# Early-fusion block on one core: queries, keys and values read back in two halves, and a new order of all engines

## The chip, the cores and the metric

The kernel runs on one core of one Trainium2 chip. The metric is the device time of one execution in microseconds (us). The core has five engines with a queue of instructions each: TensorE (PE: matmuls; its weight loads are PEld), VectorE (DVE), ScalarE (ACT), GpSimd (POOL) and SyncE (SP). In this kernel SP issues every DMA, all on one hardware queue (q1), and nothing else. An engine works through its instructions in the order written and waits on semaphores; one late instruction holds up all behind it.

## The reference, cut to what matters

```
for each of 64 images x (3, 224, 224) and texts txt (77, 256):
    p = 196 patches of 16 x 16 x 3 = 768 numbers
    h = layernorm(layernorm(p) @ W(768, 256) + b)        # 196 tokens
    h = concat(h, txt)                                   # 273 tokens of 256
    y = layernorm(h);  q, k, v = y Wq', y Wk', y Wv' + biases     # 256 each
    q, k, v of an image are split by reshape/transpose into n = 16 heads of d = 16:
        scores = einsum('nqhd,nkhd->nhqk', Q, K) / 4
        # h is a token position here: each token has its own 16 x 16 table over heads
    o = softmax(scores) V;  h = h + reshape(o) Wo' + bo
    z = layernorm(h);  z_prev = z shifted by one token
    out = h + sigmoid(mix_r(z, z_prev) Wr') * (relu(mix_k(z, z_prev) Wk')^2 Wv')
```

The attention is thus a small 16 x 16 problem for each of the 17,472 tokens, with the 16 heads as rows. All data is float32; the large products are made from a rounded part and a remainder ("hi" and "lo", three matmuls for each of two halves of the 256 inputs: six in a product).

## The kernel before, in words

The 64 images are worked on in 16 groups of four (a quad). A quad has 1092 tokens, and these are cut into three chunks of 364 tokens (CPQ = 3), each held as three tiles of 126, 126 and 112 rows (TOK, TILES). Image stages (patches to tokens) run once an image, the others once a chunk.

Everything is one software pipeline. The table AT gives each kind of step a number of due times, in units of a schedule in which a quad is 12,000 units, an image 3,000 (PERIOD of IMAGE_OPS) and a chunk 4,000. Each engine's body walks through all due times in rising order (STEPS) and issues what is due, for whichever quad it belongs to (`due`). So AT is nothing but the order of the instructions on each engine: a due time starts nothing, semaphores do. BANK says which of the eight PSUM banks each TensorE step writes; `turn` makes the step wait for the last reader of the step before it on that bank.

The steps that matter here, for a chunk k, with their names in AT and their lines:

- `qkv` (line 1066 through `product`): six products, two for each tile, into PSUM; `qb` (line 866, DVE) adds the bias and writes them to the tile qkvt.
- `qkv_out` (line 526, SP): three DMAs, one a tile, each when its two `qb` are done, from qkvt to qkv_dram in DRAM.
- `qk_in` (line 532, SP): one DMA of 768 KB reads queries and keys back, 128 bytes at a time, in an order in which partitions hold (token, head). Before it SP waits until all three tiles have landed in DRAM (`after_all(qkv_out, ...)`) and until the steps of the chunk before have read the tile qk.
- `v_in` (line 542, SP): eight DMAs of 48 KB read the values back, 64 bytes at a time.
- `kspread` (line 954, ACT, four instructions) and `qplace` (line 852, DVE, two) read the whole tile qk; then `s` (line 1103, PE, two parts) makes the scores. `mx`, `sub` (DVE), `exp` (ACT), `pt` (line 1111, PE), `ptc` (ACT), `av` (line 1124, PE; it needs all eight `v_in`), `rec`, `osb` (line 777, DVE) follow.
- `o_out` (line 547, SP): nine DMAs write the result of a chunk to o_dram; `o_in` (line 556, SP): four DMAs read it back as rows, after `o_out` of the same chunk and, for the first two chunks of a quad, of the next one has landed. `ont` (line 1180, PE) transposes the rows, `wo` multiplies.
- Other steps on SP's queue: `load` (line 495, an image), `txt` (508), `hdma` (519: three or four DMAs, the patch tokens to their place), `out` (563).
- Other steps on PE: `x` (1134), `tok` (1146), `stat` (1153), `xt` (1162), `zt` (1194), `k`, `r`, `val`, `wo` (all 1066).

The order on SP around the read-back, in the middle chunk window (due times 4653 to 7932) is: qkv_out of tile 0, out x2, txt, load, qkv_out of tile 1, o_out, qkv_out of tile 2, hdma, o_in, qk_in, out, v_in.

Of the kernel before, what the change touches and what calls it, by code (L numbers as in the profile page):

```python
# [25 lines left out]
HEADS, HD = 16, 16  # L26
IPQ, CPQ = 4, 3
QUADS = IMAGES // IPQ
# [4 lines left out]
TILES = 3  # L33
PT = 98
QKV = 3 * HD
# [6 lines left out]
BLK = 24  # L42
CTP = 16 * BLK
GR = 2 * BLK
RUN = 48
PARTS = 2
# [3 lines left out]
VROW = 5 * HD  # L50

SLOT, IMG, QUAD = 4000, 3000, 12000
AT = dict(load=[0], xcols=[1318, 1320, 1583], sq=[3246], ssq=[3924], sqm=[3700, 4330], x=[2170, 2293, 2490],
    xh=[2282, 2545, 2674], xl=[2509, 2936, 2943], tok=[3277, 4254], stat=[4432], statc=[4602], statr=[4742],
    rstd1=[4804], txt=[8554], yn=[5075, 5247], st2=[6518, 6589], mv2=[6765, 6814], rstd2=[7194], hg=[6861, 7595],
    h=[7598, 7865], hdma=[9448], st3=[12882, 13196, 13294], mv3=[13054, 13295, 13379], rstd3=[13763], xn=[14260,
    14279, 14449], xt=[14661, 15107], xnh=[14950, 15196], xnl=[15072, 15505], hb=[16159], qkv=[15721, 15888, 16255,
    16593, 16786, 17092], qb=[15897, 15942, 16599, 16651, 16997, 17149], qkv_out=[16653, 18001, 18379],
    qk_in=[18794], v_in=[19932], qplace=[19665, 19706], kspread=[19343, 19395, 19463, 19541], s=[20021, 20045],
    mx=[20102, 20201], sub=[20221, 20230], exp=[20322, 20464], pt=[20333, 20499], ptc=[20595, 20603, 20609, 20634],  # L60
    av=[20708, 20712], rec=[20736, 20809], osb=[20791, 20828], o_out=[22086], o_in=[26611], ont=[26722, 26748],
    onh=[26894, 26987], onl=[26996, 27109], wo=[27468, 27507, 27713], h2=[27696, 27736, 27802], st4=[28277, 28291,
    28297], mv4=[28302, 28428, 28473], rstd4=[28576], z=[28737, 28819, 28831], zt=[28864, 28875], carry=[27865],
    ztc=[29110, 29174], d=[29450, 29454], edge=[29465], mix=[29564, 29767, 30411, 30536], mixh=[29773, 30169, 31589,
    31775], mixl=[30115, 30183, 32095, 32294], k=[30531, 30872], kr=[30870, 31114], ksq=[30967, 31291], kah=[31781,
    32685], kal=[32727, 33437], r=[32763, 33240, 33705], rt=[32972, 33579, 33931], val=[33604, 33790, 34157],
    rv=[33858, 33944, 34175], add=[34793, 35351, 35382], out=[35541, 37270, 37274], sqh=[3466])

BANK = dict(x=[5, 3, 1], tok=[3, 1], stat=[5], yn=[7], xt=[2, 0], qkv=[0, 5, 0, 2, 5, 0], s=[4, 2], pt=[4, 6],
    av=[4, 6], ont=[5, 4], wo=[4, 6, 2], zt=[4, 6], k=[0, 6], r=[0, 2, 2], val=[0, 5, 0])  # L70
# [116 lines left out]
def fusion_kernel(nc, x, txt, ln1_g, ln1_b, tok_w, tok_b, ln2_g, ln2_b, wq, bq, wk, bk, wv, bv, wo, bo,  # L187
                  w_r, w_k, w_v, mu_r, mu_k, out):
    with ExitStack() as ctx:
# [3 lines left out]
        def sig(name, per, primed=False, unit=1):  # L193
            return Signal(ctx, nc, name, per, CPQ, primed, unit)
# [19 lines left out]
        xcols = sb("xcols", [XROWS, GRID * 128])  # L214
# [3 lines left out]
        rstd1 = sb("rstd1", [PT, 2])  # L218
# [4 lines left out]
        mv2 = sb("mv2", [PT, 2, 2])  # L223
# [20 lines left out]
        osb = probs  # L244

        mx = sb("mx", [128, BLK // 4 * 8])
# [4 lines left out]
        z = sb("z", [TT, TILES, E])  # L251
# [4 lines left out]
        kr = dT  # L256
# [3 lines left out]
        r = sb("r", [TT, TILES, E])  # L260
# [6 lines left out]
        qkv_dram = nc.dram_tensor("qkv_dram", (CPQ, CTP, HEADS, QKV), F32, kind="Internal").ap()  # L267
# [7 lines left out]
        prep_pool = ctx.enter_context(nc.semaphore("prep_pool"))  # L275
# [32 lines left out]
        st3 = sig("st3", 3)  # L308
# [5 lines left out]
        xn_lo = sig("xn_lo", 2)  # L314
        qkv_pe = sig("qkv_pe", 6, True)
        qkv_sb = sig("qkv_sb", 6)
        qkv_out = Own(ctx, nc, "qkv_out", [TILES] * CPQ, 16)
        qk_in = sig("qk_in", 1, True, unit=16)
        v_in = sig("v_in", 8, True, unit=16)
        hb_sb = sig("hb_sb", 1, True)  # L320
        q_sb = sig("q_sb", 2, True)
        kb_sb = sig("kb_sb", 4, True)
# [6 lines left out]
        av_pe = sig("av_pe", PARTS, True)  # L329
# [48 lines left out]
        def place(kind, j):  # L378
            return banks[BANK[kind][j]]

# [73 lines left out]
        def _(sp):  # L454
# [25 lines left out]
            def after(signal, q, k, steps):  # L480
                signal.wait(sp, q, k, steps)
                settle(sp)

            def after_all(own, q, k):
                own.wait(sp, q, k)
                settle(sp)

            def body(q):
                for s in STEPS:
# [30 lines left out]
                    for i, (o, rows) in enumerate(TOK):  # L520
                        for k in due(q, s, "qkv_out", i):
                            after(qkv_sb, q, k, 2 * i + 2)
                            if i == 0:
                                after(qk_in, q, k - CPQ, 1)
                                after(v_in, q, k - CPQ, 8)
                            qkv_out.done(k, sp.dma_start(qkv_dram[k % CPQ, o:o + rows, :, :].rearrange("t i j -> t (i j)"), qkvt[0:rows, i, :]))
                    for k in due(q, s, "qk_in", 0):
                        after_all(qkv_out, q, k)
                        after(kb_sb, q, k - 1, 4)
                        after(q_sb, q, k - 1, 2)  # L530
                        src = qkv_dram[k % CPQ, :, :, 0:2 * HD]
                        qk_in.done(sp.dma_start(qk[:, :, :], src.rearrange("(g t) i j -> (t i) g j", t=8)))
                    for k in due(q, s, "v_in", 0):
                        if q * CPQ + k == 0:
                            sp.wait_ge(prep_pool, POOL_ALL)
                        after_all(qkv_out, q, k)
                        after(av_pe, q, k - 1, PARTS)
                        src = qkv_dram[k % CPQ, :, :, 2 * HD:QKV].rearrange("(r g y) i j -> r y i g j", r=2, y=4)
                        for rr in range(2):
                            for yy in range(4):  # L540
                                p = 64 * rr + HEADS * yy
                                v_in.done(sp.dma_start(vb[p:p + HEADS, :, yy, 0:HD], src[rr, yy]))
# [21 lines left out]

            quads(sp, body)
            out_dma.wait(sp, QUADS - 1, CPQ - 1, 3)
            qk_in.wait(sp, QUADS - 1, CPQ - 1, 1)
            v_in.wait(sp, QUADS - 1, CPQ - 1, 8)
            on_in.wait(sp, QUADS - 1, CPQ - 1, ROW_DMAS)

# [135 lines left out]
        def _(dve):  # L706
# [42 lines left out]
            def body(q):  # L749
                for s in STEPS:  # L750
# [93 lines left out]
                            mv3_sb.done(V.bn_aggr(mv3[0:rows, i, :], bn3[0:rows, i, :]))  # L844
                    for xx in range(2):
                        for k in due(q, s, "qplace", xx):
                            qk_in.wait(dve, q, k, 1)
                            s_pe.wait(dve, q, k - 1, PARTS)
                            settle(dve)
                            half = slice(64 * xx, 64 * xx + 64)  # L850

                            q_sb.done(V.tensor_reduce(qx[half, :, xx, :], qk[half, :, 0:HD].unsqueeze(3), AX.X, ALU.max))  # L852
# [4 lines left out]
                    for job in range(6):  # L857
                        for k in due(q, s, "qb", job):
                            i, half = job // 2, job % 2
                            rows = TOK[i][1]  # L860
                            qkv_pe.wait(dve, q, k, job + 1)
                            if job == 0 and q * CPQ + k == 0:
                                dve.wait_ge(prep_act, ACT_ALL)
                            if job == 0:
                                qkv_out.wait(dve, q, k - 1)
                            qkv_sb.done(V.tensor_tensor(qkvt[0:rows, i, NQ * half:NQ * half + NQ], place("qkv", job)[0:rows, 0:NQ],  # L866
                                                        bqkv[0:rows, :, :].rearrange("p i j -> p (i j)")[:, NQ * half:NQ * half + NQ], ALU.add))

# [48 lines left out]
        def _(act):  # L917
# [319 lines left out]
```

## Time and profile before

| | us |
|---|---|
| median of 3 runs | 1610.56 (1608.76 to 1613.27) |
| the profiled execution's own time | 1609.15 |
| its span, first to last instruction | 1607.4 |

| engine | busy us | share of the span |
|---|---|---|
| PE | 1450.4 | 90% |
| PEld | 1378.2 | 86% |
| DVE | 1264.3 | 79% |
| ACT | 1113.4 | 69% |
| POOL | 947.0 | 59% |

The profile's page gives busy times of each engine, their course over the span, the DMA queues, the chain of work that ended last, and groups of like instructions with the idle time of the engine before them and what ended it ("releaser"). "issue" as a releaser means that nothing the profile shows was waited for.

### The profile page before, as it was taken

Reading aid. Unit: us, or ns where it says so; the run is one execution under the profiler, and the core shown is the slowest. Engines: PE = TensorE matmul, PEld = TensorE weight load, DVE = VectorE, ACT = ScalarE, POOL = GpSimd, SP = SyncE. Lnnn points to the kernel's source line nnn. Section 1 sums busy time; section 2 is a strip of 40 time slices with the busy share of each in tenths; the row PEclk is TensorE's granted clock in tenths of the full one; section 3 lists DMA queues with packets and bytes.
Section 4 is the critical chain, followed back from the end, with each engine's and each line's share of the span. In section 5 each row is a group of like instructions: output and inputs, shape, how many; then the busy total and the mean of one; then the engine's idle time right before and its main releaser. Section 6 shows DMA issues by size and latency. Waiting matters only on the chain.

```text
span 1607.4 us, 53715 instructions
## 1 busy us (share of the span) xinstructions
PE 1450.4 (90%) x18762; PEld 1378.2 (86%) x18762; DVE 1264.3 (79%) x3171; ACT 1113.4 (69%) x2230; POOL 947.0 (59%) x1428
## 2 busy tenths in 40 slices
PE   4687899999989999998999899999999999897866
PEld 4676899899989999898989899998988999897755
DVE  5566798888888888887988688888888788886753
ACT  4554687777777787776777678777777777765643
POOL 3342376566667666565667566666766566664546
PEclk8788899999999999999999999999999999999998
DMA  5267987997878887987888798798888689868760
GB/s 140 63 125 126 139 154 147 150 159 158 151 144 162 157 156 154 149 152 145 155 147 157 140 151 154 162 150 147 155 158 156 137 152 148 160 123 127 123 100 29
DMA packets 702660, 227.67 MB, mean 142 GB/s; under 512 B 617470, under 2 KB 673854, under 8 KB 702394
## 3 DMA queue, kind: packets, MB, share of 16 engines
q1 hardware_dynamic: 702394, 224.23, 77.3%
q8 instruction: 153, 2.51, 0.8%
q14 instruction: 113, 0.93, 0.3%
HBM read 121.64 MB, written 89.64 MB: 131 GB/s over the span
## 4 chain that ended last, share of the span: by engine, by line
PE 65%; SPq 8%; issue 6%; DMA 5%; DVE 3%; POOL 1%; ACT 1%; DVEq 0%; POOLq 0%; ACTq 0%
PE bank L1066 33%; PE bank L1146 13%; PE bank L1103 4%; PE bank L1124 4%; SPq L547 4%; DMA qk<-qkv_dram 3%; PE bank L1134 3%; SPq L519 2%; PE bank L1111 2%; PE bank L1180 2%; PE bank L1162 1%; PE bank L1194 1%; DMA on<-o_dram 1%; SPq L556 1%; PE bank L1153 1%
## 5 line engine op out<-in xcount | busy, mean ns | idle before, releaser
L1066 PE MATMUL bank<-wqkv,xnT 128*126 128x384 f32 (+1 forms) x1728 | 357.8, 347 | 6.9 <-issue 6.8
L1146 PE MATMUL bank<-wtok,xT 128*98 128x258 f32 x2304 | 315.7, 293 | 13.3 <-DVE xT L789 9.3
L1146 PEld LDWEIGHTS bank<-wtok,xT 128*98 128x98 f32 x2304 | 294.8, 172 | 18.9 <-DVE xT L789 11.3
L1066 PEld LDWEIGHTS bank<-wqkv,xnT 128*126 128x126 f32 (+1 forms) x1728 | 293.6, 186 | 10.6 <-issue 8.0
L689 POOL TENSOR_TENSOR mixp<-mixf,mixp 128x364 fp32r<-128x364 f32 x192 | 185.5, 977 | 166.0 <-ACT mixp L1040 158.7
L866 DVE TENSOR_TENSOR qkvt<-bank,bqkv 126x384 f32<-126x384 f32 (+1 forms) x288 | 156.0, 550 | 83.5 <-PE bank L1066 83.4
L954 ACT ACTIVATE arena<-qk,ymask 128x768 f32<-128x768 f32 x192 | 164.0, 926 | 57.1 <-DMA qk<-qkv_dram 56.9
L637 POOL TENSOR_TENSOR xcols<-xcols 84x896 f32<-84x896 f32 x59 | 124.9, 2117 | 86.9 <-ACT xcols L996 86.3
L987 ACT ACTIVATE xT<-bank 128x420 fp32r<-128x420 f32 (+1 forms) x192 | 100.5, 536 | 61.7 <-PE bank L1134 59.9
L1066 PE MATMUL bank<-wrT,mixp 128*126 128x256 f32 (+1 forms) x864 | 134.3, 292 | 4.8 <-POOL mixp L689 2.9
L979 ACT ACTIVATE xcols<-xim 84x640 f32<-84x640 f32 (+1 forms) x192 | 126.5, 694 | 12.9 <-DVE xs L784 12.0
L626 POOL TENSOR_TENSOR rs<-ve,small 126x3 f32<-126x3 f32 (+1 forms) x160 | 127.7, 798 | 12.5
L852 DVE TENSOR_REDUCE qx<-qk 64x768 f32<-64x768 f32 x96 | 90.8, 945 | 54.2 <-DMA qk<-qkv_dram 52.7
L899 DVE SCALAR_TENSOR_TENSOR mixf<-dT,mus,bank 128x364 f32<-128x364 f32 x192 | 110.1, 584 | 21.3 <-POOL dT L683 17.1
L1066 PE MATMUL bank<-mixp,wkfT 128*128 128x364 f32 x576 | 120.3, 345 | 5.6 <-POOL mixp L689 5.0
L1066 PEld LDWEIGHTS bank<-wrT,mixp 128*126 128x126 f32 (+1 forms) x864 | 114.8, 186 | 10.2 <-POOL mixp L689 3.8
L1066 PE MATMUL bank<-wvfT,kaT 128*126 128x256 f32 (+1 forms) x864 | 121.9, 285 | 1.2 <-DVE r L911 0.9
L1134 PE MATMUL bank<-ident,xcols 84*128 84x84 f32 x896 | 100.4, 246 | 24.1 <-DVE bank L808 13.0
L1066 PE MATMUL bank<-woT,onT 128*126 128x256 f32 (+1 forms) x864 | 117.3, 287 | 2.2 <-DVE onT L872 2.2
L642 POOL TENSOR_TENSOR var<-stat,mean 98x2 f32<-98x2 f32 x64 | 12.6, 197 | 176.4 <-DVE stat L799 176.4
L966 ACT ACTIVATE pt<-bank 64x384 f32<-64x384 f32 x192 | 93.1, 485 | 33.1 <-PE bank L1111 29.6
L677 POOL TENSOR_TENSOR dT<-zT 128x364 f32<-128x364 f32 x96 | 74.1, 794 | 69.5 <-ACT zT L1034 69.5
(125 smaller groups left out, 3328.4 us busy)
## 6 DMA issues: line engine op xcount, KB each, us to landing
xim<-in_x SPq DMA_DIRECT2D x128, 294.0 KB
qk<-qkv_dram SPq DMA_DIRECT2D x48, 768.0 KB, 7.7
qkv_dram<-qkvt SPq DMA_DIRECT2D x96, 378.0 KB
arena<-qkv_dram SPq DMA_DIRECT2D x384, 48.0 KB
qkv_dram<-qkvt SPq DMA_DIRECT2D x48, 336.0 KB
o_dram<-probs SPq DMA_DIRECT2D x288, 48.0 KB, 1.8
out<-h SPq DMA_DIRECT2D x96, 126.0 KB
on<-o_dram SPq DMA_DIRECT2D x64, 126.0 KB
```

What stands on the lines that cost most here:

```text
L626: done.done(P.tensor_tensor(rs[:, :], ve[:, :], powt[0:part, 0:ve.shape[1]], ALU.pow))
L637: x_half.done(P.tensor_tensor(halves[:, 0, :, :], halves[:, 0, :, :], halves[:, 1, :, :], ALU.add))
L689: mix_lo.done(P.tensor_tensor(mixp[:, w, 1, kk, :], mixf[:, kk, :], mixp[:, w, 0, kk, :].bitcast(F32), ALU.subtract))
L866: qkv_sb.done(V.tensor_tensor(qkvt[0:rows, i, NQ * half:NQ * half + NQ], place("qkv", job)[0:rows, 0:NQ], bqkv[0:rows, :, :].rearrange("p ...
L899: mix_sb.done(V.scalar_tensor_tensor(out=mixf[:, kk, :], in0=dT[:, kk, :], scalar=mus[:, w, kk:kk + 1], in1=place("zt", kk)[:, 0:CT], op0= ...
L954: kb_sb.done(A.activation(kb[:, :, yy, :], qk[:, :, HD:2 * HD], ACT.Copy, scale=ymask[:, yy:yy + 1]))
L966: pt_sb.done(A.activation(pt2[64 * rr:64 * rr + 64, PB * part:PB * part + PB, :, rr, :], place("pt", part)[64 * rr:64 * rr + 64, 0:32 * PB ...
L979: x_cols.done(A.activation(xcols[:, 128 * w0:128 * w1].rearrange("p (w r q) -> p w r q", r=HALF, q=PS), xim[:, :].rearrange("p (r w q) -> ...
L987: x_hi.done(A.activation(xT[:, 0, :, w0:w1], src, ACT.Copy))
L1066: ins = mm(psum, left(a, k), right(b, k), start=t == 0, stop=t == len(terms) - 1)
L1134: ins = tr(place("x", job)[:, XROWS * (w - w0):XROWS * (w - w0) + XROWS], xcols[:, 128 * w:128 * w + 128], ident[0:XROWS, 0:XROWS])
L1146: ins = mm(place("tok", c)[0:PT, 0:E + 2], xT[:, a, i0:i0 + GRID // 2, :].rearrange("p i w -> p (i w)"), wtok[:, b, ch, :], start=t == 0, ...
```

## The change

Four edits, and one that goes over everything:

1. The signal of the write-out is split: qkv_out counts tiles 0 and 1, a new qkv_end counts tile 2.
2. `qk_in` becomes two DMAs of 384 KB, with a due time each. The first reads tokens 0 to 191 of the chunk and waits only for tiles 0 and 1 (tokens 0 to 251) in DRAM; the second reads the rest and waits for tile 2 too. `kspread` and `qplace` wait for both.
3. `v_in` becomes two steps of four DMAs each, with the same waits.
4. `qb` of the next chunk waits for qkv_end as well.
5. Every due time in AT and nearly every bank in BANK is another. On SP the read-back is now, in the middle chunk window (4643 to 7126): qkv_out of tile 0, txt, qkv_out of tile 1, o_out, qkv_out of tile 2, qk_in first half, o_in, qk_in second half, hdma, load, v_in first half, out, v_in second half. On TensorE, from `av` of a chunk to the `ont` of the chunk before it, the order is r0, qkv4, zt, qkv5, x and r1, val0, r2, val1, val2, tok, k0, xt0, ont in this window before; it is qkv4, r0, qkv5, zt, x and r1, r2, val0 to val2, tok, k0, xt0, xt1, k1, ont after. From qkv5 to the first `s` of the same chunk both orders hold two tok, stat, three val, two r, one image's x, two k, two xt, two ont and two qkv; before there are also three wo, after two wo and two zt.

```
-    st3=[12882, 13196, 13294], ... qkv=[15721, 15888, 16255, 16593, 16786, 17092],
-    qb=[15897, 15942, 16599, 16651, 16997, 17149], qkv_out=[16653, 18001, 18379],
-    qk_in=[18794], v_in=[19932], qplace=[19665, 19706], kspread=[19343, 19395, 19463, 19541], s=[20021, 20045],
-    ... av=[20708, 20712], rec=[20736, 20809], osb=[20791, 20828], o_out=[22086], o_in=[26611], ont=[26722, 26748],
+    st3=[11805, 11903, 12190], ... qkv=[14573, 14584, 14947, 15304, 15637, 16016],
+    qb=[14667, 14706, 15296, 15397, 15916, 16032], qkv_out=[16643, 17110, 17292],
+    qk_in=[17362, 17672], v_in=[18137, 19126], qplace=[18505, 18524], kspread=[18429, 18432, 18448, 18484], s=[18755, 18760],
+    ... av=[19360, 19636], rec=[19684, 19745], osb=[19748, 19752], o_out=[21202], o_in=[25473], ont=[26050, 26162],
...
-        qkv_out = Own(ctx, nc, "qkv_out", [TILES] * CPQ, 16)
-        qk_in = sig("qk_in", 1, True, unit=16)
+        qkv_out = Own(ctx, nc, "qkv_out", [2] * CPQ, 16)
+        qkv_end = Own(ctx, nc, "qkv_end", [1] * CPQ, 16)
+        qk_in = sig("qk_in", 2, True, unit=16)
...
-                            qkv_out.done(k, sp.dma_start(...))
-                    for k in due(q, s, "qk_in", 0):
-                        after_all(qkv_out, q, k)
-                        after(kb_sb, q, k - 1, 4)
-                        after(q_sb, q, k - 1, 2)
-                        src = qkv_dram[k % CPQ, :, :, 0:2 * HD]
-                        qk_in.done(sp.dma_start(qk[:, :, :], src.rearrange("(g t) i j -> (t i) g j", t=8)))
-                    for k in due(q, s, "v_in", 0):
-                        ...
-                        for rr in range(2):
+                            (qkv_out if i < 2 else qkv_end).done(k, sp.dma_start(...))
+                    for rr in range(2):
+                        for k in due(q, s, "qk_in", rr):
+                            after_all(qkv_out, q, k)
+                            if rr:
+                                after_all(qkv_end, q, k)
+                            else:
+                                after(kb_sb, q, k - 1, 4)
+                                after(q_sb, q, k - 1, 2)
+                            src = qkv_dram[k % CPQ, CTP // 2 * rr:CTP // 2 * rr + CTP // 2, :, 0:2 * HD]
+                            qk_in.done(sp.dma_start(qk[:, BLK * rr:BLK * rr + BLK, :], src.rearrange("(g t) i j -> (t i) g j", t=8)))
+                        for k in due(q, s, "v_in", rr):
+                            ...
+                            after_all(qkv_out, q, k)
+                            if rr:
+                                after_all(qkv_end, q, k)
+                            else:
+                                after(av_pe, q, k - 1, PARTS)
...
-                            qk_in.wait(dve, q, k, 1)
+                            qk_in.wait(dve, q, k, 2)
...
+                                qkv_end.wait(dve, q, k - 1)
...
-                                qk_in.wait(act, q, k, 1)
+                                qk_in.wait(act, q, k, 2)
```

## Rows read from the trace of the kernel before

**Rows 1.** The page's head and its first part: busy us (share) xinstructions.
```profile
span 1607.4 us, 53715 instructions
...
PE 1450.4 (90%) x18762; PEld 1378.2 (86%) x18762; DVE 1264.3 (79%) x3171; ACT 1113.4 (69%) x2230; POOL 947.0 (59%) x1428
```
**Rows 2.** Busy time by stretch: start, middle and end of the run, columns in the first line.
```profile
core 0: us, PE busy (x) PEld busy (x) DVE busy (x) ACT busy (x) POOL busy (x), PEclk, DMA share, GB/s
0.00:200.00 200.00, 143.31 (x1422) 134.51 (x1423) 123.95 (x298) 101.25 (x185) 68.83 (x124) 0.85 0.63 119
200.00:1400.00 1200.00, 1144.29 (x15319) 1094.20 (x15318) 1013.26 (x2563) 898.37 (x1805) 764.78 (x1137) 0.99 0.84 152
1400.00:1608.00 208.00, 162.82 (x2023) 149.47 (x2022) 127.13 (x312) 113.81 (x242) 113.43 (x168) 0.95 0.58 104
```
**Rows 3.** Waits of PE, 200 to 1400 us: waiting <- releaser: us, times, longest.
```profile
PE bank L1180 <- DMA on<-o_dram: 17.5, 12, 2.2
PE bank L1103 <- issue: 16.9, 21, 2.5
PE bank L1124 <- issue: 6.3, 5, 3.7
```
**Rows 4.** The chain that ended last, 700 to 760 us: start us, us, what.
```profile
722.28 0.99 PE bank L1124 x46
...
725.16 0.31 SPq L547
...
728.84 0.42 SPq L547
729.38 0.36 SPq L526
729.99 0.79 SPq L519
...
734.38 0.33 SPq L556
...
735.61 2.11 DMA on<-o_dram
737.76 0.85 PE bank L1180 x6
```
**Rows 5.** SP's timeline, 686 to 725 us: start us, us, engine line op out<-in xcount.
```profile
699.81 0.35 SPq L526 DMA_DIRECT2D qkv_dram<-qkvt  x1
...
701.06 1.47 SPq L556 DMA_DIRECT2D on<-o_dram  x4
702.79 0.40 SPq L532 DMA_DIRECT2D qk<-qkv_dram  x1
```
**Rows 6.** What reads and writes the tile qk, 200 to 1400 us: durations, landing.
```profile
L954 ACT ACTIVATE arena<-qk,ymask x159: 917/922/945, 199.6 to 1395.2; 128x768 f32<-128x768 f32 x159
...
DMA to landing us min/median/max: 6.9/7.7/9.1
```
**Rows 7.** The chain that ended last, whole run: lengths of TensorE steps.
```profile
396.64 2.15 PE bank L1146 x18
398.79 2.82 PE bank L1066 x24
```
**Rows 8.** The chain that ended last, 1470 to 1540 us (the end of the run).
```profile
1478.29 7.49 DMA qk<-qkv_dram
...
1493.60 1.05 PE bank L1066 x6
...
1501.62 2.77 DMA qkv_dram<-qkvt
1504.62 7.13 DMA qk<-qkv_dram
...
1531.73 7.36 DMA qk<-qkv_dram
```
**Rows 9.** The page's DMA issues: KB each, median us from issue to landing.
```profile
o_dram<-probs SPq DMA_DIRECT2D x288, 48.0 KB, 1.8
```

More of the change, by code:

```diff
@@ L52 @@
 SLOT, IMG, QUAD = 4000, 3000, 12000
[L53 to L58, printed above, removed]
-    qk_in=[18794], v_in=[19932], qplace=[19665, 19706], kspread=[19343, 19395, 19463, 19541], s=[20021, 20045],
[L60 to L67, printed above, removed]
@@ L69 @@
-BANK = dict(x=[5, 3, 1], tok=[3, 1], stat=[5], yn=[7], xt=[2, 0], qkv=[0, 5, 0, 2, 5, 0], s=[4, 2], pt=[4, 6],
-    av=[4, 6], ont=[5, 4], wo=[4, 6, 2], zt=[4, 6], k=[0, 6], r=[0, 2, 2], val=[0, 5, 0])
+AT = dict(load=[0], xcols=[520, 575, 1066], sq=[2536], ssq=[3118], sqm=[3504, 3521], x=[1147, 1315, 1348], xh=[1421,
+    1534, 1605], xl=[1448, 1769, 1827], tok=[2216, 3215], stat=[3306], statc=[3506], statr=[3613], rstd1=[3700],
+    txt=[7688], yn=[4137, 4156], st2=[5150, 5471], mv2=[5563, 5770], rstd2=[6383], hg=[5727, 6031], h=[6728, 6763],
+    hdma=[8728], st3=[11805, 11903, 12190], mv3=[12254, 12268, 12276], rstd3=[12632], xn=[13144, 13351, 13481],
+    xt=[13692, 13813], xnh=[14049, 14278], xnl=[14107, 14384], hb=[15441], qkv=[14573, 14584, 14947, 15304, 15637,
+    16016], qb=[14667, 14706, 15296, 15397, 15916, 16032], qkv_out=[16643, 17110, 17292], qk_in=[17362, 17672],
+    v_in=[18137, 19126], qplace=[18505, 18524], kspread=[18429, 18432, 18448, 18484], s=[18755, 18760], mx=[18861,
+    18872], sub=[18895, 18925], exp=[18987, 18991], pt=[19233, 19257], ptc=[19242, 19347, 19413, 19415], av=[19360,
+    19636], rec=[19684, 19745], osb=[19748, 19752], o_out=[21202], o_in=[25473], ont=[26050, 26162], onh=[26402,
+    26403], onl=[26434, 26441], wo=[26666, 26669, 26764], h2=[26729, 26735, 26999], st4=[26993, 27168, 27178],
+    mv4=[27220, 27370, 27373], rstd4=[27544], z=[27683, 27999, 28012], zt=[28056, 28139], carry=[26769], ztc=[28231,
+    28367], d=[28462, 28467], edge=[28473], mix=[28600, 28704, 29385, 29598], mixh=[28788, 29167, 29790, 30510],
+    mixl=[29008, 29318, 30623, 30661], k=[29621, 29919], kr=[29913, 30290], ksq=[30095, 30339], kah=[30632, 30820],
+    kal=[31056, 31667], r=[31922, 32308, 32469], rt=[32103, 32591, 32942], val=[32785, 32962, 33004], rv=[32834,
+    33076, 33162], add=[33724, 34252, 34312], out=[34720, 35795, 36432], sqh=[2880])
@@ L71 @@
+BANK = dict(x=[5, 1, 3], tok=[1, 3], stat=[5], yn=[7], xt=[5, 6], qkv=[6, 0, 4, 6, 0, 2], s=[5, 0], pt=[2, 0],
+    av=[2, 4], ont=[4, 0], wo=[4, 2, 6], zt=[6, 4], k=[0, 2], r=[5, 0, 2], val=[5, 0, 2])
 BANK_ORDER = ("s", "pt", "av", "x", "tok", "stat", "xt", "qkv", "ont", "wo", "zt", "k", "r", "val", "yn")
@@ L523, in body @@
                             if i == 0:
-                                after(qk_in, q, k - CPQ, 1)
+                                after(qk_in, q, k - CPQ, 2)
                                 after(v_in, q, k - CPQ, 8)
-                            qkv_out.done(k, sp.dma_start(qkv_dram[k % CPQ, o:o + rows, :, :].rearrange("t i j -> t (i j)"), qkvt[0:rows, i, :]))
-                    for k in due(q, s, "qk_in", 0):
-                        after_all(qkv_out, q, k)
-                        after(kb_sb, q, k - 1, 4)
-                        after(q_sb, q, k - 1, 2)
-                        src = qkv_dram[k % CPQ, :, :, 0:2 * HD]
-                        qk_in.done(sp.dma_start(qk[:, :, :], src.rearrange("(g t) i j -> (t i) g j", t=8)))
@@ L533, in body @@
-                    for k in due(q, s, "v_in", 0):
[L534 to L538, printed above, removed]
-                        for rr in range(2):
+                            (qkv_out if i < 2 else qkv_end).done(k, sp.dma_start(qkv_dram[k % CPQ, o:o + rows, :, :].rearrange("t i j -> t (i j)"), qkvt[0:rows, i, :]))
@@ new lines, in body @@
+                    for rr in range(2):
[9 more added lines that the diff above has]
+                        for k in due(q, s, "v_in", rr):
+                            if q * CPQ + k == 0:
+                                sp.wait_ge(prep_pool, POOL_ALL)
+                            after_all(qkv_out, q, k)
[3 more added lines that the diff above has]
+                                after(av_pe, q, k - 1, PARTS)
+                            src = qkv_dram[k % CPQ, :, :, 2 * HD:QKV].rearrange("(r g y) i j -> r y i g j", r=2, y=4)
@@ L566, in _ @@
             out_dma.wait(sp, QUADS - 1, CPQ - 1, 3)
-            qk_in.wait(sp, QUADS - 1, CPQ - 1, 1)
+            qk_in.wait(sp, QUADS - 1, CPQ - 1, 2)
             v_in.wait(sp, QUADS - 1, CPQ - 1, 8)
```

## The prediction

> **What bounds the kernel now.** I read the page's busy shares first: TensorE is busy 90% of the span, VectorE 79%, ScalarE 69% [rows 1]. That is an average over three parts, so next come the sums by stretch [rows 2]. Between 200 and 1400 us TensorE is busy 1144 of 1200 us at a granted clock of 0.99; only 56 us are idle there. Before 200 us it idles 57 us at a clock of 0.85, and after 1400 us 45 us at 0.95. So the run is TensorE-bound with 158 us of holes, and a change that removes no matmul can win at most part of these. The DMA engines are busy 84% of the middle [rows 2], the second thing to watch.
>
> Then the waits of TensorE in the middle [rows 3]: 17.5 us before the transposes of `ont`, for the read-back of the attention result, and 16.9 us before the scores `s`, 21 times, put down to "issue"; 6.3 us before `av`. The first two, 34.4 us, are 2.6 us in each of the 13 quads of about 90 us. The scores need the tile qk whole, and its readers on ScalarE and VectorE stand between. One transfer takes 7.7 us in the median to land (6.9 to 9.1) [rows 6]; then four ScalarE instructions of 0.92 us, 3.7 us [rows 6], then `s`.
>
> The chain shows why both are late once a quad [rows 4]: `av` ends at 723.3, the nine `o_out` issues run on SP from 725.2 to 729.3, `qkv_out` of the last tile takes 0.36, then come four `hdma` issues from 730.0 to 734.2, four `o_in`, 2.1 us of landing, and `ont` starts at 737.8. SP's queue is the path here, and `qk_in` stands behind all that.
>
> **The change part by part.** All times are against the profiled execution: span 1607.4, own time 1609.15, thus 1.7 us around the span; the median, 1610.56, is 1.4 above it.
>
> (a) The first half no longer waits for the last tile in DRAM. In a window without `hdma` the last tile's write is issued at 699.81 and `qk_in` at 702.79, 3.0 us later [rows 5]; at the end of the run the write lands in 2.77 us [rows 8]. In these 3 us the first half can now move. How much of the landing is fixed? The nearest small transfer, 48 KB to DRAM, lands in 1.8 us [rows 9]; with that as the fixed part of 7.7, the 768 KB cost 5.9 and half of it 3.0, so the second half lands 4.8 us after its issue instead of 7.7. The gain is 2.9 us, if the first half is through in the 3 us, which it just is; I take 2.7, the write it hides under. The bounds: 0 (the queue is busy anyway, as the 84% say) and 3.9 (half of 7.7, no fixed part).
> The Trainium skill, in DMA: Bandwidth & Descriptors, section "Anatomy of one DMA", gives a DMA about 2 us fixed plus its bytes at 436 GB/s (measured there on GpSimd's path). By that 768 KB would land in 3.8 us and half in 2.9, and splitting would win 0.9 only. The trace's 7.7 us disagrees: pieces of 128 bytes make this transfer costlier than its bytes, so I keep 2.7; by the page's figures the end of the run under (d) would win 2.7 in place of 8.
>
> (b) The order on SP. `hdma` goes from before `o_in` and `qk_in` to after both, 4.2 us of issues (730.0 to 734.2) off the path of that window [rows 4]. In exchange `qk_in`'s first half stands before `o_in`: 0.4 us of issue [rows 5], and 3 us of its packets ahead of `o_in`'s on the same queue, of which 1.5 pass while `o_in`'s four DMAs are being issued [rows 5]. One issue more a chunk is 48 x 0.4 = 19 us of SP over the run, inside its idle time. The waits added are no new events: `o_out`, queued before both halves, already makes SP wait for VectorE's `osb`.
>
> (c) The order on TensorE. I add up the steps between producer and consumer. 18 matmuls of `tok` take 2.15; 24 of `r`, `val`, `wo` 2.82, so 0.71 a product [rows 7]; a product of `qkv` or `k` 1.05 [rows 8]; a transpose group 0.3 (0.85 for the six of `ont` [rows 4], part of it start-up). From the last `qkv` to the first `s`: 4.3 (tok) + 0.3 + 2.1 (val) + 1.4 (r) + 1.2 (x) + 2.1 (k) + 0.6 + 0.6 + 2.1 (qkv) = 14.7, and 2.1 for three `wo` before, against 1.4 + 0.6 after: 16.8 and 16.7. So the chunk's path through DRAM gets no more cover than before; it has to become shorter itself, and (a) and (b) do that. From `av` to `ont` the cover grows by `xt1` and `k1`, 0.3 + 1.05 = 1.3 us.
>
> Now the two waits. For `ont` in the window with `hdma`: av end to ont start was 14.5 (723.3 to 737.8) [rows 4]; minus 4.2 for `hdma`, plus 0.4, plus 0 to 3 behind the first half (1.5 is what (b) leaves), makes 10.7 to 13.7, against a cover of 11.8 + 1.3 = 13.1 (11.8 is the same sum for the old order: 0.7 r, 2.1 qkv, 0.6 zt, 1.2 x, 1.4 r, 2.1 val, 2.15 tok, 1.05 k, 0.3 xt, rounded up for starts). A stall of 0 to 0.6 in place of 1.5 us. In the window without `hdma` [rows 5], where no wait was left, the same 0.4 to 3.4 come on top and 1.3 of cover; that may cost up to 1 us once a quad. For `s`: the read-back ends 2.7 us sooner in all windows and up to 4 more where `hdma` went; what `o_in`'s packets between the halves take back is under 1 us. The stalls are 1 to 2 us a quad, so nearly all should go. Of the 34.4 us I take two thirds as gone, 23 us, because two ends meet closely at `ont`. Bounds: 34 gone; or 34 stay.
>
> (d) The end and the start. After 1400 us the DMA of qk stands three times in the chain, 7.49, 7.13 and 7.36 us [rows 8]: nothing covers it there, and each loses the 2.7 us of (a): 8 us. Bounds 0 and 12 (3 x 3.9). In the first 200 us the image stages set the pace; the depth of the pipeline changes from 37,274 to 36,432 units, 2%, of which most is only the first `xcols` standing 800 units nearer its load. I take 0, within 10 either way, which is some fifth of the 57 us idle there.
>
> (e) All other distances. A new order of some 550 steps a quad can open a hole anywhere. I compared the TensorE work in front of each step: `zt` behind `wo` loses 2.6 us, `k` behind `zt` 1.0, `tok` behind `x` of one image 2.1; others gain or stay. These chains run over VectorE, GpSimd and ScalarE, which have 16 to 36% idle time in the middle [rows 2]. I take 0; a hole of 0.5 us a chunk would cost 24 us, the reordering at its best wins the 6.3 us before `av` too [rows 3].
>
> The sum: 1607.4 - 23 - 8 = 1576.4, plus 1.7 around the span 1578, plus 1.4 to the median: 1580 us.
>
> **The rivals.** R1, *the queue, not the wait, is the limit*: the DMA engines have 84% of the time work [rows 2], and the first half merely moves its packets ahead of `o_in`'s, so that the second half lands when the whole did. Then only the `hdma` move pays: 4.2 us of path once a quad, of which 1.5 reach TensorE, over 13 quads 19 minus 5 for `ont` late in the other window: about 1597. For it: the 84%. Against: SP spaces them, the write's 3 us were idle for this chunk. DMA: Bandwidth & Descriptors, section "Queues, rings and completion order" of the Trainium skill says that an engine takes descriptors in ring order; that is what R1 needs, and the landing of 6.9 to 9.1 with other transfers issued behind it [rows 6] agrees.
> R2, *slower*: `ont` becomes late in two windows of three. Place: `o_in` behind the first half of qk. Price: if the half holds the queue for 6 us, of which 1.5 pass under `o_in`'s issues, `ont` starts at 14.5 - 4.2 + 0.4 + 4.5 = 15.2 against 13.1, 2.1 us late in 32 of 48 chunks: 67 us, less the 31 won, 1610.6 + 36 = 1647. It decides from the point where the lateness is 1.0 us (32 x 1.0 = the 31 won): a half that holds the queue for 4.9 us instead of 3.0. For it: the spread of the landings, 6.9 to 9.1. Against: half the packets can hardly take longer than two thirds of the whole.
> R3, *the order wins more*: both waits go whole (34), with the 6 before `av`, 12 at the end and 5 at the start: 1610.6 - 57 = 1554. The trace says that these are all short waits of 1 to 2 us [rows 3], which favours it; against it that something is always next.
> R4, *no change*: the new holes of (e) eat the gain: 1608.
>
> **How the numbers follow.** Forecast (1570 to 1592) 0.50, R1 0.16, R2 0.10, R3 0.12, R4 and small losses 0.12. The predicted time is the forecast's 1580. The range goes from 1562, which leaves out half of R3, to 1612, which takes in R1 and R4 and leaves out R2: 1562 to 1612. What a measurement can tell from no change is 0.3%, 5 us. Faster: 0.50 + 0.16 + 0.12 and a little of R4 = 0.79; same 0.10 (from R4); slower 0.11 (R2 and the rest of R4).
>
> **What would show it.** After: the waits of TensorE at lines 1103 and 1180 in the middle at a third of 34.4 us; busy share there up from 95% to 97%; landing of a half of qk near 4.8 us where nothing is ahead; in the chain of the last 200 us shorter pieces of qk; the first half issued right after the last tile's write, the second some 3 us later. Wrong if the second half lands over 10 us after the write's issue (R1), if the wait at `ont` is above 20 us (R2), or if a line that now waits for nothing (`zt`, `k`, `tok`) has over 10 us before it (R4).

## The result, and the profile after

The changed kernel takes 1641.38 us (median of 4 runs, 1633.49 to 1647.78) against 1609.66 for the kernel before, measured beside it: ratio 1.0184, 95% interval [1.0142, 1.0227]. It is slower by 1.8%; I had forecast 1580, faster.

The profiled execution took 1641.83 us with a span of 1640.1, 32.7 more than before. The sums by stretch of the changed kernel, same columns as [rows 2]:

```profile
0.00:200.00 200.00, 145.68 (x1545) 136.56 (x1546) 130.81 (x314) 106.47 (x197) 73.56 (x131) 0.86 0.63 120
200.00:1400.00 1200.00, 1109.77 (x14910) 1070.48 (x14912) 980.91 (x2492) 868.28 (x1757) 743.04 (x1110) 0.99 0.81 149
1400.00:1641.00 241.00, 192.12 (x2321) 179.74 (x2312) 148.55 (x367) 131.88 (x278) 127.27 (x188) 0.92 0.58 105
```

TensorE's busy time in all is nearly the same (1447.6 us, 1450.4 before); in the middle it idles 90 us where it idled 56, at the same clock of 0.99. Start and end idle 54 and 49 us (57 and 45 before). So the loss is in the steady state. The page's chain of work that ended last says where to look: SP's issues are 29% of it where they were 8%, TensorE 36% where it was 65%. The waits of TensorE in the middle, to hold against [rows 3]; line 1133 is `av`, 1189 `ont`, 1112 `s`, 1120 `pt`, 1075 the products:

```profile
PE bank L1133 <- issue: 24.2, 13, 2.7
PE bank L1189 <- DMA on<-o_dram: 23.8, 25, 2.5
PE bank L1112 <- issue: 19.6, 16, 2.1
PE bank L1133 <- ACT pt L975: 8.7, 11, 1.1
PE bank L1075 <- issue: 8.1, 6, 2.5
PE bank L1120 <- ACT probs L968: 5.2, 7, 1.4
```

The wait before `av` went from 6.3 to 24.2 us, that before `ont` from 17.5 to 23.8 and from 12 to 25 times, and that before the scores, which was to go, from 16.9 to 19.6. (3.7 of the 6.3 us before are one hole inside a group of `av`, at 909 us; what caused it is not shown.) One `av` that waits, on SP and on TensorE (start us, us, ..., idle before in brackets):

```profile
628.91 2.87 SPq L550 DMA_DIRECT2D arena<-qkv_dram  x4
631.96 0.37 SPq L571 DMA_DIRECT2D out<-h  x1
632.60 3.31 SPq L520 DMA_DIRECT2D hc<-yh  x4
636.04 1.93 SPq L496 DMA_DIRECT2D xim<-in_x  x2
638.15 3.13 SPq L550 DMA_DIRECT2D arena<-qkv_dram  x4
```
```profile
644.40 1.68 PE L1133 MATMUL bank<-arena,pt 128*32 128x68 f32 x96 [1.97 <-issue]
```

The first four transfers of the values are out at 631.8, the second four start at 638.2, because `out`, four `hdma` and `load` stand between the halves. The last is issued at 641.3 and `av` starts 3.1 us later, after 2.0 us of nothing.

Another stretch of SP in the changed kernel, the window of a chunk with k mod 3 = 1, to hold against [rows 4, 5]; then the end of the `av` of the chunk before, on TensorE:

```profile
860.90 3.12 SPq L520 DMA_DIRECT2D hc<-yh  x3
864.16 0.90 SPq L496 DMA_DIRECT2D xim<-in_x  x2
865.17 0.32 SPq L527 DMA_DIRECT2D qkv_dram<-qkvt  x1
865.68 5.00 SPq L555 DMA_DIRECT2D o_dram<-probs  x9
870.79 0.70 SPq L527 DMA_DIRECT2D qkv_dram<-qkvt  x1
871.74 1.34 SPq L538 DMA_DIRECT2D qk<-qkv_dram  x1
873.27 3.23 SPq L564 DMA_DIRECT2D on<-o_dram  x4
876.68 0.38 SPq L538 DMA_DIRECT2D qk<-qkv_dram  x1
```
```profile
860.89 1.68 PE L1133 MATMUL bank<-arena,pt 128*32 128x68 f32 x96 [1.12 <-ACT pt L975]
```

Two things are to be seen. `av` ends at 862.6 but `o_out` starts at 865.7, 3.1 us later, since SP is still busy with `hdma` and `load`; what stands behind it is late too. Both stood ahead of `o_out` in this window before the change as well, but SP was through with them before `av` ended. This is SP in the kernel before, in a window of the same kind; the `av` ends at 848.4 us:

```profile
842.80 1.33 SPq L495 DMA_DIRECT2D xim<-in_x  x2
844.24 0.77 SPq L563 DMA_DIRECT2D out<-h  x2
845.26 2.51 SPq L519 DMA_DIRECT2D hc<-yh  x3
847.89 0.49 SPq L526 DMA_DIRECT2D qkv_dram<-qkvt  x1
849.64 5.33 SPq L547 DMA_DIRECT2D o_dram<-probs  x9
```

And the four `o_in` take 3.2 us to issue where they took 1.5 [rows 5]: the first half of qk is ahead of them. A half lands in 5.5 us in the median, later than the forecast 4.8 (first the tile qk in the middle, then the page's list):

```profile
DMA to landing us min/median/max: 4.4/5.5/6.9
```
```profile
qk<-qkv_dram SPq DMA_DIRECT2D x96, 384.0 KB, 5.5
qkv_dram<-qkvt SPq DMA_DIRECT2D x48, 336.0 KB, 3.2
```

From the semaphore events of the same traces, medians over ten chunks of each kind, us after the end of `av` of the chunk before:

| k mod 3 | kernel | o_out starts | last qkv_out | qk all landed | `s` starts | values landed | `av` starts |
|---|---|---|---|---|---|---|---|
| 0 | before | 1.2 | 6.0 | 19.8 | 23.9 | 26.1 | 29.9 |
| 0 | after | 1.4 | 5.6 | 15.9 | 20.6 | 28.0 | 28.4 |
| 1 | before | 1.2 | 5.8 | 16.3 | 20.8 | 24.9 | 27.4 |
| 1 | after | 2.8 | 8.1 | 19.3 | 23.1 | 25.1 | 30.4 |
| 2 | before | 1.1 | 6.2 | 17.7 | 21.3 | 28.1 | 28.4 |
| 2 | after | 1.4 | 5.7 | 16.4 | 20.6 | 29.4 | 29.6 |

In one window the read-back gained 3.9 us (there `hdma` and `o_in` stood ahead of it), in another it lost 3.0. The waits of TensorE in the middle, sorted by these windows, follow the table: before `av` 21.3 us in k mod 3 = 2 and 9.9 in 0 (the rows with "issue" and with ACT together), before `ont` 16.6 of the 23.8 in k mod 3 = 1, before `s` 15.3 of the 19.6 there too.

### The profile page after: what moved, and what is told of

It is laid out like the page before. It is cut to its first block, busy times and chain, and to the rows that moved or that the text cites. A ratio compares the mean times of both kernels' runs of the same rounds, so it can differ in the third digit from the quotient of the medians.

```text
span 1640.1 us, 53961 instructions
## 1 busy us (share of the span) xinstructions
PE 1447.6 (88%) x18762; PEld 1386.8 (85%) x18762; DVE 1260.3 (77%) x3171; ACT 1106.6 (67%) x2230; POOL 943.9 (58%) x1428
## 4 chain that ended last, share of the span: by engine, by line
PE 36%; SPq 29%; issue 10%; DMA 10%; DVE 3%; POOL 2%; ACT 2%; DVEq 0%; POOLq 0%; ACTq 0%
PE bank L1075 17%; SPq L555 8%; PE bank L1155 7%; SPq L564 7%; SPq L550 5%; SPq L520 5%; PE bank L1133 3%; PE bank L1112 3%; DMA on<-o_dram 3%; DMA qk<-qkv_dram 3%; DMA o_dram<-probs 2%; DMA arena<-qkv_dram 2%; SPq L496 1%; PE bank L1143 1%; PE bank L1189 1%
## 5 line engine op out<-in xcount | busy, mean ns | idle before, releaser
L1155 PE MATMUL bank<-wtok,xT 128*98 128x258 f32 x2304 | 310.4, 290 | 10.2 <-DVE xT L797 10.2
L1155 PEld LDWEIGHTS bank<-wtok,xT 128*98 128x98 f32 x2304 | 290.7, 170 | 12.6 <-DVE xT L797 12.1
L988 ACT ACTIVATE xcols<-xim 84x640 f32<-84x640 f32 (+1 forms) x192 | 131.0, 696 | 63.1 <-DMA xim<-in_x 34.2
L1075 PE MATMUL bank<-wrT,mixp 128*126 128x256 f32 (+1 forms) x864 | 129.0, 293 | 6.3 <-issue 4.3
L1075 PE MATMUL bank<-woT,onT 128*126 128x256 f32 (+1 forms) x864 | 123.0, 287 | 6.1 <-DVE onT L881 3.5
L1075 PEld LDWEIGHTS bank<-woT,onT 128*126 128x126 f32 (+1 forms) x864 | 110.3, 184 | 13.4 <-issue 5.2
L797 DVE TENSOR_TENSOR xT<-bank,xT 128x420 fp32r<-128x420 f32 (+1 forms) x192 | 102.9, 558 | 21.7 <-ACT xT L996 21.4
L1133 PE MATMUL bank<-arena,pt 128*32 128x68 f32 x4608 | 85.5, 228 | 37.6 <-issue 27.3
L1075 PE MATMUL bank<-wvfT,kaT 128*126 128x256 f32 (+1 forms) x864 | 113.1, 283 | 3.8 <-ACT r L1063 3.8
L1133 PEld LDWEIGHTS bank<-arena,pt 128*32 128x32 f32 x4608 | 77.4, 111 | 45.7 <-issue 27.9
```

What stands on the lines that cost most here:

```text
L988: x_cols.done(A.activation(xcols[:, 128 * w0:128 * w1].rearrange("p (w r q) -> p w r q", r=HALF, q=PS), xim[:, :].rearrange("p (r w q) -> ...
L1075: ins = mm(psum, left(a, k), right(b, k), start=t == 0, stop=t == len(terms) - 1)
L1133: ins = mm(place("av", part)[32 * j:32 * j + 32, col:col + AVW], pt2[:, b, xx, :, :].rearrange("p r q -> p (r q)"), vrow[:, g, 0:AVW], sta ...
L1155: ins = mm(place("tok", c)[0:PT, 0:E + 2], xT[:, a, i0:i0 + GRID // 2, :].rearrange("p i w -> p (i w)"), wtok[:, b, ch, :], start=t == 0, ...
```

## The experiments

All run on one chip at a time beside the kernel before, whose medians were 1606 to 1614 us; ratios are to it. The runs e, f and g were taken on three chips, so between these groups the ratios compare better than the medians. "Old order" is the AT of before, "new order" that of the change. The first theory after the result: the loss comes from places on SP's queue, above all the second half of the values (A), not from the split (B) nor from the other engines' new order (C).

**e1, only the split, old order.**
```
-    qk_in=[18794], v_in=[19932]      (code of the change, AT and BANK of before)
+    qk_in=[18794, 18796], v_in=[19932, 19933]
```


> The old order of everything, with only the read-back split: both halves of qk where the one transfer stood (due 18794 and 18796), both halves of v where it stood. Theory A (the loss comes from where the new order puts things on SyncE's queue, the split by itself gains a little): in the windows without hdma the last write is out 3.0 us before qk_in, so the first half gains up to 1.5 us of start; some of the 16.9 us before the scores goes; 1598 to 1609 us. Rival B (the split itself costs: one more transfer a chunk, halves that land in 5.5 us instead of 3.9): slower than before by more than 5 us, 1616 or more.

Measured: 1607.59 us, ratio 1.0006 [0.9964, 1.0047]. B falls: halves that stand where the whole stood cost nothing, and gain nothing either, within the 0.4% (7 us) of the interval. It is in A's range, at its end.

**e2, the new order without the split.**
```
-    qk_in=[17362, 17672], v_in=[18137, 19126]      (code of before, AT and BANK of the change)
+    qk_in=[17672], v_in=[18137]
```


> The new order with the read-back whole: one qk_in where the second half stood (17672, behind o_in), all eight v_in where the first four stood (18137). Theory A: the wait before av (24 us in the middle of the changed kernel) goes because no v piece stands behind hdma, load and out, and the wait before ont (24 us) goes because o_in has no half of qk ahead of it; the scores may wait up to 0.5 us a chunk more. 1641 - 32 - 30 + 20 = about 1600, at least under 1615. Rival B (split costs): 1600 too, but then the next kernel, which has the split, stays far above it. Rival C (the new order of TensorE and the others is what costs): stays at 1630 or more.

Measured: 1657.58 us, 1.0323 [1.0245, 1.0401]. A's number was wrong by 58 us, and the range of C (1630 or more) is the one it fell in. In the middle the waits of TensorE are:

```profile
PE bank L1103 <- issue: 64.5, 31, 5.0
...
PE bank L1180 <- DMA on<-o_dram: 1.1, 2, 0.7
```

The waits before `av` and `ont` went as A said, but the scores (line 1103 here) wait 64.5 us. So the new order has a fault of its own, which the split partly makes good.

Long waits cost a second time here, through TensorE's clock. At each of the eleven longest waits before the scores in the middle of e2 a stretch at half clock (0.50, the level of 1.2 GHz) starts within 2.1 us of the wait's end. The longest wait ends at 1286.0 us (columns of [rows 2]):

```profile
1281.00:1286.00 5.00, 0.00 (x0) 0.01 (x1) 3.29 (x6) 3.49 (x5) 0.00 (x0) 0.85 0.73 63
1286.00:1291.00 5.00, 4.98 (x105) 4.83 (x106) 3.86 (x10) 2.96 (x8) 1.93 (x2) 0.50 0.45 116
```

The granted clock is 0.97 over the middle of e2 against 0.99 in the changed kernel, and TensorE is busy 1462.0 us in all for the same work against 1447.6.

**e3, the change with the halves of v together.**
```
-    v_in=[18137, 19126]
+    v_in=[18137, 18138]
```


> The changed kernel with one due time altered: the second half of v right behind the first (18138 instead of 19126), so ahead of out, hdma and load. Theory A: the wait before av, 24.2 us in the middle and some 2.9 us a quad by the signals, goes; 16 x 2.9 = 46 us, but part is handed to the next wait: 1595 to 1612. Theory A2 (ont behind the first half of qk is the main cause): 1630 to 1641, since ont still waits. Rival C: 1635 or more.

Measured: 1619.85 us, 1.0095 [1.0051, 1.0140], 8 us above A's range and below those of A2 and C; against the change 0.9 points by the ratios (14 us; the two intervals just miss each other), 22 us by the medians. Waits in the middle:

```profile
PE bank L1189 <- DMA on<-o_dram: 27.8, 24, 3.6
PE bank L1112 <- issue: 15.2, 13, 1.8
...
PE bank L1133 <- issue: 3.0, 2, 1.5
```

24.2 us before `av` became 3.0. This one due time is about half of the loss by the ratios (14 of 30 us), two thirds by the medians. What is left sits in the window k mod 3 = 1: 21.6 of the 27.8 us before `ont` and 13.9 of the 15.2 before `s`. Against e2, which differs only by the split and the place of its first half ahead of `o_in`, e3 is 2.3 points faster.

**e4, old order, `o_in` and the whole `qk_in` moved ahead of `hdma`.**
```
-    qk_in=[18794], o_in=[26611]
+    qk_in=[18410], o_in=[26400]
```


> The old order and the whole read-back, with only o_in (26400) and qk_in (18410) moved to right behind the last qkv_out, ahead of hdma and txt. Theory A (SyncE's queue behind o_out is the path in the window with hdma): the 17.5 us wait before ont and most of the 16.9 before the scores go, 1610 - 30 = 1580, anywhere in 1575 to 1592. Rival D (a transfer queue that is busy 84% gives nothing for an earlier issue): within 5 us of 1610.

Measured: 1594.57 us, 0.9929 [0.9889, 0.9970], 3 us above A's range; D, within 5 us of 1610, is out. The waits before the scores and, in the last row, before `ont` are down to this:

```profile
PE bank L1103 <- DVE qx L852: 6.7, 10, 0.8
...
PE bank L1103 <- issue: 2.5, 2, 2.3
...
PE bank L1180 <- DMA on<-o_dram: 1.4, 2, 0.8
```

That is 24 us of waits less, for 0.7 points or 11 us of time; products and `av` show 17.8 us of "issue" instead of 9.3. The execution that was profiled took 1606.02 us, 11 more than the median. It is the part (b) of the change without its exchange.

**f1, e4 with the first half of qk ahead of `o_in`.**
```
-    qk_in=[18410], v_in=[19932]      (on e4, with the code of the change)
+    qk_in=[18390, 18410], v_in=[19932, 19933]
```


> e4 (old order, o_in and qk_in right behind the last qkv_out) with the read-back split and the first half of qk ahead of o_in (18390, o_in 26400, second half 18410), as the change has it. Theory A (a half of qk ahead of o_in makes the attention rows 2.3 us later: 6.1 us from issue to landing in the changed kernel, 3.8 without): the rows land at 13.3 and 14.3 us after av, ont could start at 12.4 and 12.2, so 0.9 + 2.1 = 3.0 us a quad come back before ont, 48 us, less some 10 before the scores: 1620 to 1640 us, the wait before ont 25 us or more in the middle. Rival C (in the old order of the other engines the half ahead is harmless): within 8 us of e4's 1595.

Measured: 1616.79 us, 1.0012 [0.9977, 1.0047], 0.8 points over e4 (13 us), 3 us under A's range. The wait is back where it was expected:

```profile
PE bank L1189 <- DMA on<-o_dram: 40.8, 34, 2.6
```

By the semaphore events `o_in` lands 6.1 us after its issue in f1 and 3.9 in e4 (3.6 to 4.2 over its windows), and the tile qk is complete 10.0 to 10.4 us after the last write's issue in f1 against 10.7 to 10.9 in e4: the split wins some 0.6 us for the scores and costs 2.2 for the rows.

**f3, e3 with `o_in` ahead of both halves.**
```
-    o_in=[25473]
+    o_in=[25355]
```


> e3 (changed kernel, both v halves together) with o_in moved ahead of both halves of qk (due 25355 instead of 25473). o_in must wait for o_out to land, 1.6 us, so the first half starts when the last write is nearly in, and the split has nothing left to hide. Theory A (the new order has one gap and two transfers that want it): the wait before ont falls from 27.8 to under 4 us in the middle, the wait before the scores rises from 15 to 45 or more, and the time is 1640 to 1660, as e2's. Rival (the late rows are a cost by themselves that can be had back): 1590 to 1600.

Measured: 1648.61 us, 1.0206 [1.0151, 1.0261]. As A said, one wait for the other (before `ont` 1.5 us are left):

```profile
PE bank L1112 <- issue: 55.1, 30, 4.8
```

**f6, e3 with the first half nearly left out.**
```
+    n = BLK if rr else 1
-    qk[:, BLK * rr:BLK * rr + BLK, :]
+    qk[:, BLK * rr:BLK * rr + n, :]
```


> e3 with nearly all of the first half of qk left out: that DMA moves 1 of its 24 groups (16 KB for 384 KB), so half of the scores are made from stale data. Everything else, the order and the number of DMAs, stays. Theory A (it is the packets of the first half that hold up the rows): from issue to landing of o_in 3.8 instead of 6.1 us, the wait before ont from 27.8 to under 6 us; the second half lands sooner too, so the wait before the scores falls as well; 1575 to 1592. Rival E (the wait before ont comes from SyncE being late, or from av being late, not from the packets): the wait before ont stays over 15 us and the time over 1605.

Measured: 1546.54 us, 0.9583 [0.9525, 0.9641], 29 us under A's range. Half of the scores are made from stale data here, so this prices a transfer and is no kernel to keep. Same number of transfers, and:

```profile
PE bank L1190 <- DMA on<-o_dram: 3.4, 3, 1.7
```

From issue to landing `o_in` takes 3.8 to 4.0 us again (6.0 to 6.4 in e3), its four issues 1.4 to 1.6 (3.2 to 3.5). So it is the packets, not the place of one more transfer. E falls. The size says what the traffic of this one half costs in all: 73 us by the medians, 82 by the ratios. 19 us of it are TensorE's busy time (1428.2 us against 1447.5 in e3, at a mean granted clock of 0.973 against 0.965).

**f5, e3 with `hdma` earlier.**
```
-    hdma=[8728]
+    hdma=[7728]
```


> e3 with hdma 1000 units earlier (7728 instead of 8728), so that hdma and load no longer stand one behind the other ahead of o_out in the same chunk window (k mod 3 = 1, where o_out starts 3.5 us after av instead of 1.4 and the last qkv_out 2.5 us later than in the other windows). Theory F (that window's score wait, 1.3 us a quad, and the wait before pt, 0.8, come from SyncE's queue ahead of o_out): both go, the wait before the scores in the middle falls from 15 to under 8, 16 x 1.5 = 24 us off 1620: 1592 to 1608. Rival: the four hdma now stand ahead of o_out in the neighbouring window and cost the same there: 1612 to 1625.

Measured: 1666.16 us, 1.0330 [1.0271, 1.0388], worse than either theory. `hdma` now came before its data: of SP's waits in the middle the first is

```profile
SPq L282 <- DVE yh L836: 55.5, 12, 9.0
```

and the wait before `ont` rose to 61.6 us. It tells nothing of F, only that a step of SP may be placed too early at a high price.

**g1 and g4, what stands ahead of `o_out`.** Both are e2 with one image's `hdma` in four left out, g1 the one ahead of `o_out` in the window k mod 3 = 1, g4 another as a control. Both compute with stale tokens. (g1 leaves out three DMAs a quad and g4 four, not the other way round as the two expectations have it, so the control takes away more.)
```
+    if m == 0:          # g4: m == 2
+        sp.sem_inc(patch_in.sems[m], patch_in.pers[m]); continue
```


> e2 (new order, whole read-back, 1658) with the hdma of the first image of each quad left out: its four DMAs, which stand with load right ahead of o_out in the window k mod 3 = 1, are replaced by a count on the semaphore, so 196 tokens of every fourth image are stale. Theory G (64.5 us before the scores in e2 come mostly from SyncE reaching o_out 3.6 us after av in that window instead of 1.4): o_out starts at 1.4, the last qkv_out 2 to 3 us sooner, the wait before the scores falls to 25 to 40 us, the time to 1605 to 1630. Rival H (any 3 us less on a queue that is busy that much would do; or the rest of the order is what costs): the time falls no more than in the control g4 below, or stays over 1640.

> Control for g1: e2 with the hdma of the third image of each quad left out (its three DMAs stand in the window k mod 3 = 2, behind the read-back, ahead of load). Same kind of work and bytes gone, at another place. Theory G: the wait before the scores stays over 50 us, the time at 1645 to 1660. Rival H: the same gain as g1.

Measured: g1 1625.86 us, 1.0092 [1.0036, 1.0147]; g4 1658.51 us, 1.0297 [1.0245, 1.0348]. Leaving out the control's four DMAs gains nothing (1.0323 in e2, the intervals overlap), leaving out the three ahead of `o_out` gains 33 us against g4, by the ratios and by the medians. Waits in the middle, g1, then g4:

```profile
PE bank L1106 <- issue: 43.8, 33, 3.2
```
```profile
PE bank L1106 <- issue: 66.9, 33, 5.1
```

In g1 `o_out` starts 1.4 us after `av` in that window and the last write is issued at 6.5; in g4 it is 3.2 and 8.6. G holds (43.8 us is above its 25 to 40): a fault of the new order is `hdma`, with `load` behind it, so close ahead of `o_out`. The clock has a share: TensorE is busy 1445.9 us in g1 and 1457.9 in g4, 12 of the 31 us between their spans. It explains some half of what e2 is over e4; the rest I did not isolate, and neither the new banks nor the new order of the other engines was tested by itself. A candidate is `wo2`, 0.7 us of work that the new order moved from before `s` to behind it.

**g2, f1 with the change's cover for `ont`.**
```
-    ont=[26722, 26748], onh=[26894, 26987], onl=[26996, 27109]
+    ont=[27112, 27114], onh=[27150, 27200], onl=[27300, 27510]
```


> f1 (old order, first half of qk ahead of o_in, 1617) with ont moved behind k1 and xt1 on TensorE, and onh and onl with it on the other engines: the 1.3 us of cover that the changed kernel has. Theory A (the half ahead makes the rows 2.3 us late and the cover decides what of it shows): the wait before ont falls from 40.8 to 10 us or less in the middle; 1585 to 1600. Rival: the work moved ahead of ont was cover for wo behind it, and the wait reappears before wo (line 1075 behind onT): 1610 or more.

Measured: 1639.50 us, 1.0189 [1.0133, 1.0244]. The rival holds: only 1.3 us of waits are left before `ont`, but in their place

```profile
PE bank L1075 <- DVE onT L881: 18.7, 13, 1.5
PE bank L1143 <- DVE onT L881: 12.6, 13, 1.0
```

the work put ahead of `ont` had covered `wo` behind it, and images' transposes (`x`, which share bank 5 with `ont`, and `ont` now holds it longer) wait too. The waits were about exchanged, 39.5 us for 31.3. That g2 is slower than f1 comes with TensorE's busy time, 1480.8 us against 1456.9, at a mean granted clock of 0.949 against 0.964.

**g3, e4 with the two `qplace` together.**
```
-    qplace=[19665, 19706]
+    qplace=[19665, 19666]
```


> e4 (old order, rows and whole qk right behind the last qkv_out, 1595) with the two qplace next to each other, so that no h2 stands between them on VectorE while the scores wait. The 6.7 us that TensorE waits for qplace in the middle go, if kspread is not right behind: 1585 to 1595. If kspread, which ends within 0.7 us of qplace, is next: same as e4 within 5 us.

Measured: 1593.18 us, 0.9894 [0.9847, 0.9942]. The 6.7 us before the scores for `qplace` are gone, but other waits there grew: 8.6 us in all (4.2 for "issue", 2.5 for `h2` on VectorE, 1.9 for `kspread`) where e4 had 9.2. The ratio is 0.35 points below e4's and the two intervals overlap, so no gain is shown. e4 and g3 both beat both kernels; what is shown to pay is e4's move of two due times.

## Why the prediction was wrong

*What bounds the kernel* held: TensorE, with holes from SP's queue. Of the 34.4 us before `ont` and `s` the forecast took 23 as gone; measured, the two rose to 43.4, and 18 more came before `av`. *Part (d)*, start: within 3 us of idle. Its end failed in size: the two pieces of qk left in the chain took 6.99 and 6.06 us where 4.4 to 4.8 was forecast (2.7 off 7.1 to 7.5), and the stretch after 1400 us idles 49 us, not 8 less than 45.

```profile
1533.91 6.99 DMA qk<-qkv_dram
...
1563.61 6.06 DMA qk<-qkv_dram
```

*Part (e)*, "I take 0", is the step that failed most. I checked TensorE's distances for zt, k, tok and not the one for `av`, whose input is not made by an engine but by SP: the change gives v_in a second place, behind out, hdma and load, and none of these was counted although all stand in SP's queue. Measured: 24.2 us of waits in the middle, 14 to 22 us of time (e3).

*Part (b)* took SP's time as free ("inside its idle time") and looked at `hdma` in one window only. In the window k mod 3 = 1 `hdma` stands ahead of `o_out` in both orders. But `o_out` moved up by 884 units, `hdma` by 720 and `load` not at all: `hdma` is 474 units ahead of `o_out` and `load` 202, where they were 638 and 1,086. SP had issued them before `av` ended; now it is still at them 2.5 us after (the stretches shown). In e2's setting that costs 33 us (g1 against g4). What it costs in the changed kernel, where the early half of qk gives slack, no run shows by itself; in its window k mod 3 = 1 `s` starts 2.3 us later than before, and most of the waits before `ont` and `s` fall there.

*Part (b)* also let 1.5 us of the half's packets fall on `o_in`. It is 2.2 us (f1 against e4: 3.9 to 6.1 us of landing), between the 1.5 and the 3 that I named as the end of the range. In the window k mod 3 = 0, where the forecast had `ont` stall for 0 to 0.6 us, it stalls for 0.3 in the mean, which is right. The window k mod 3 = 1, where "up to 1 us" was allowed, has 1.3 us, because `av`'s results are written out late there.

*Part (a)* took 4.8 us for a half and 2.7 us of gain. A half lands in 5.5, and the last write in 3.2 instead of 2.8 us with the half beside it. With `o_in` between the halves the tile is complete only 0.6 us sooner than a whole transfer behind `o_in` (f1 against e4). The 3 us beside the write were not idle: `o_in` used them. That is R1's mechanism, which I had at 0.16. The sign that I named for it came true: the second half lands 10.2 to 11.2 us after the write's issue, over the 10. The Trainium skill, DMA: Bandwidth & Descriptors, section "Queues, rings and completion order", says that an engine takes descriptors in ring order. The traces agree: the rows land in 3.9 us without and in 6.1 us with the half ahead (e4 and f1).

*Part (c)* measured the scores' cover from the last `qkv`. The chain begins earlier, at the `av` of the chunk before, through `osb`, nine `o_out` and the last write, as [rows 4] already showed. Measured from there the new order has less cover. By the terms of part (c) the work from `av` to `s` is 0.7 us shorter (`wo2`); in the traces the earliest `s` of the middle starts 20.7 us after `av` in the kernel before and 19.8 in the changed one, so the path through DRAM had to become that much shorter only to keep up.

*R2* gave the sign and, at 1647, nearly the time, and its mark, a wait at `ont` above 20 us, came true with 23.8. That the time is so near is luck: its mechanism, `ont` late by 2.1 us in two windows, is only part. The wait before `ont` rose by 6 us in the middle, that before `av` by 18.

## What to carry to other kernels

Where one in-order queue issues all transfers, list its whole order before and after and put each consumer's wait against the last transfer it needs; a chain's cover is counted from where the chain starts, here SP's previous block of nine issues, not from the producer of the data. Look at what stands close ahead of such a block, too: the same steps ahead of it cost nothing while the queue got through them in time. A transfer split to use a gap takes the gap from what uses it now, and whether that pays depends on which of the two has less cover: the same split was worth -2.3 points in one order (e3 against e2), +0.8 in another (f1 against e4) and 0 where its neighbours stayed (e1).

## What the runs showed of the hardware

A transfer ahead on the queue holds up not only what lands after it but also the engine that issues: four `o_in` took 1.5 us to issue, and 3.2 us with 384 KB in pieces of 128 bytes ahead, most of the difference in the first. With 16 KB in such pieces ahead it was 1.4 to 1.6 us again (f6). No run varied the size of the pieces. The chain that ended last has the first issue alone, the timeline all four:

```profile
714.56 2.08 SPq L564
```
```profile
714.56 3.20 SPq L564 DMA_DIRECT2D on<-o_dram  x4
```

Halving the bytes cut the median landing of the read-back only from 7.7 to 5.5 us; each half had other transfers beside it, the last write or `o_in`. And idle time of TensorE cost clock in these runs: in e2 it fell to 0.50 within 2.1 us of the end of each of the eleven longest waits before the scores (the longest, 5.0 us, is shown above).
